# Attention turns of two rounds: the order of copies, maxima and query projections changed, and constant matmuls put into the start

## The reference, cut to what matters

```python
x = x + tanh(g_xattn[0]) * L0_xattn(layernorm(x), ctx)   # cosine similarities of two projections
x = x + tanh(g_ffn[0])   * L0_ffn(layernorm(x))          # ternary weights, rows quantised to 8 bits
x = x + tanh(g_xattn[1]) * L1_xattn(layernorm(x), ctx)   # the stage that is changed
x = x + tanh(g_ffn[1])   * L1_ffn(layernorm(x))          # 8 bit weights, one scale for the whole tensor
```

```python
q = layer_norm(x) @ Wq;  k, v = split(ctx @ Wkv)         # 16 heads, one null key and value in front
attn = softmax((q * s) @ (k * s).T, masked)              # 128 x 129 per head and batch
out  = layer_norm((attn @ v).reshape(b, 128, 1024) @ Wout)
```

## Time and profile before

| | us |
|---|---|
| three runs | 321.82, 320.54, 321.28 (median 321.28) |
| the profiled execution, its own time | 321.2 |
| its span | 319.4 |
| PE busy | 288.1 (90%) |
| DVE busy | 256.3 (80%) |
| ACT busy | 237.7 (74%) |
| POOL busy | 157.8 (49%) |
| chain that ended last, by engine | PE 37%, DVE 26%, ACT 18%, issue 7%, POOL 6% |

### The profile page before, as it was taken

One profiled execution on the slowest core, in us unless ns is written; L12 is line 12 of the kernel. 1 busy time (PEld: TensorE's weight loads), 2 busy tenths in 40 slices (PEclk: granted clock), 3 DMA queues, 4 the chain that ended last, 5 costly groups with the idle time before them and its releaser, 6 DMA issues.

```text
span 319.4 us, 7701 instructions
## 1 busy us (share of the span) xinstructions
PE 288.1 (90%) x2594; PEld 238.7 (75%) x2594; DVE 256.3 (80%) x730; ACT 237.7 (74%) x811; POOL 157.8 (49%) x225
## 2 busy tenths in 40 slices
PE   7988999999999848999998998989999998977765
PEld 6767768686767637889998998989889887842455
DVE  3798999999886446667887888988889889858875
ACT  2777696869899665898888897888978886419290
POOL 2124617342442114645578797867857586443200
PEclk9999999999999995999999999999999999999999
DMA  5741000002020000000000000000000000000004
GB/s 156 180 127 27 1 25 3 3 0 66 3 66 3 0 0 0 2 3 3 0 3 2 2 1 3 2 0 3 3 3 2 1 2 2 1 2 0 1 2 131
DMA packets 11479, 6.67 MB, mean 21 GB/s; under 512 B 3825, under 2 KB 10993, under 8 KB 11441
## 3 DMA queue, kind: packets, MB, share of 16 engines
q1 hardware_dynamic: 10560, 5.99, 6.9%
q10 hardware_dynamic: 880, 0.20, 0.3%
HBM read 5.14 MB, written 1.05 MB: 19 GB/s over the span
## 4 chain that ended last, share of the span: by engine, by line
PE 37%; DVE 26%; ACT 18%; issue 7%; POOL 6%; DMA 3%; SPq 2%; ACTq 0%; DVEq 0%; POOLq 0%
PE psum L1074 10%; DVE rmx L2023 9%; ACT work L1005 8%; PE psum L1078 6%; PE psum L1080 5%; PE psum L1079 5%; DVE den L2038 3%; POOL work L584 3%; DVE work L2016 2%; ACT late L1005 2%; DMA KT<-in_L_ffn_w_down 2%; DVE hgm L2221 2%; ACT work L1065 2%; PE psum L1539 2%; PE psum L1202 2%
## 5 line engine op out<-in xcount | busy, mean ns | idle before, releaser
L584 POOL TENSOR_TENSOR work<-work,rden 128x512 f32<-128x512 f32 x51 | 52.9, 1040 | 43.3 <-DVE rden L2042 43.3
L1005 ACT ACTIVATE work<-psum,nmx 128x128 f32<-128x128 f32 x208 | 73.3, 383 | 0.0
L1074 PE MATMUL psum<-ident,work 128*128 128x128 f32 (+2 forms) x328 | 49.9, 285 | 7.1 <-DVE work L2016 4.8
L1074 PEld LDWEIGHTS psum<-ident,work 128*128 128x128 f32 (+2 forms) x328 | 37.5, 145 | 16.1 <-issue 8.8
L1005 ACT ACTIVATION_READ_ACCUMULATOR work<-psum,nmx 128x1 f32 x208 | 46.7, 225 | 0.0
L2023 DVE TENSOR_REDUCE rmx<-psum 128x8 f32<-128x1024 f32 x32 | 38.6, 1208 | 5.0 <-PE psum L1202 5.0
L1202 PE MATMUL psum<-KT,work 64*128 64x128 f32 x512 | 35.5, 288 | 5.9 <-ACT work L1005 5.0
L2038 DVE SCALAR_TENSOR_TENSOR den<-null_exp,masked,key_sum 128x4 f32<-128x4 f32 x64 | 22.6, 353 | 20.6 <-ACT work L1005 15.9
L1202 PEld LDWEIGHTS psum<-KT,work 64*128 64x128 f32 x512 | 31.9, 193 | 9.1 <-issue 8.1
L1078 PE MATMUL psum<-split 128*128 128x256 f32 (+1 forms) x96 | 37.3, 389 | 1.3 <-issue 0.8
L1080 PE MATMUL psum<-split 128*128 128x256 f32 (+1 forms) x96 | 31.0, 323 | 0.0
(11 more groups left out here) (216 smaller groups left out, 757.4 us busy)
## 6 DMA issues: line engine op xcount, KB each, us to landing
KT<-in_L_xattn_Wkv SPq DMA_DIRECT2D x2, 384.0 KB, 4.7
X<-in_x SPq DMA_DIRECT2D x1, 768.0 KB, 5.8
out_x<-X SPq DMA_DIRECT2D x3, 256.0 KB, 2.6
work<-in_ctx SPq DMA_DIRECT2D x3, 192.0 KB, 2.4
work<-in_L_xattn_Wq SPq DMA_DIRECT2D x1, 512.0 KB, 3.6
work<-in_L_xattn_Wout SPq DMA_DIRECT2D x1, 512.0 KB, 3.9
X<-in_x SPq DMA_DIRECT2D x1, 256.0 KB, 3.5
KT<-in_L_ffn_w_gate SPq DMA_DIRECT2D x1, 256.0 KB, 5.7
```

Source lines behind the costliest of these rows:

```text
L584: pool.tensor_tensor(sx_, sx_, bcast(rden[n % 2][:, :], S), ALU.mult).then_inc(p_ready.sem, 1)
L1005: ins = act.activation(Sx[n % 5][:, j, :], bank[2 * (r % 2) + j % 2][:, at * S:(at + 1) * S], ACT.Exp, bias=nmx[r % 2][:, col:col + 1], ac ...
L1074: return pe.transpose(dst, src, ident[0:m, 0:m])
```

## The change

On PE, the second query projection of a turn now stands in front of the odd transposes. On DVE, the maxima of the odd round stand behind the copies of the even transposes of the next turn, and both copies of the odd transposes stand in front of the denominator of unit new + 1. In turn 0 and turn 1, PE gets 22 and 2 constant matmuls, and the transposes of round 0 move from turn 2 into turn 1. In the last turn one `pair_work` moves behind the last copies.

```diff
             for M in range(NT + 1):
-                both(round_transposes, 2 * M - 4)
+                if M > 2:
+                    both(round_transposes, 2 * M - 4)
                 queries(2 * M)
                 both(out_proj, 2 * M - 6)
+                queries(2 * M + 1)
                 both(round_transposes, 2 * M - 3)
-                queries(2 * M + 1)
                 both(out_proj, 2 * M - 5)
...
                 both(round_scores, 2 * M)
+                if M == 1:
+                    keep_clock_long(bank[5], 2)
+                    both(round_transposes, 0)
                 both(round_scores, 2 * M + 1)
+                if M == 0:
+                    keep_clock_long(bank[5], 22)
...
                     p_evac(old + 1)
                 if new >= 0:
+                    maxima(2 * M - 1)
                     denominators(new)
                 if old >= 0:
                     p_evac(old + 2)
+                    p_evac(old + 3)
                 if new >= 0:
                     denominators(new + 1)
-                if old >= 0:
-                    p_evac(old + 3)
                 if M == NT:
                     p_evac(NS - 4)
                 pair_work(2 * M)
                 if new >= 0:
                     denominators(new + 2)
-                pair_work(2 * M + 1)
+                if M < NT:
+                    pair_work(2 * M + 1)
                 if new >= 0:
                     denominators(new + 3)
                 if M < NT:
                     maxima(2 * M)
-                    maxima(2 * M + 1)
             last_normalise()
             p_evac(NS - 3)
             p_evac(NS - 2)
+            pair_work(2 * NT + 1)
```

## The result

The changed kernel takes 332.85 us in the median of four runs, against 321.55 for the kernel before beside it; the ratio is 1.0263, with a 95% interval from 1.0167 to 1.0359. Two of the four runs were disturbed ones, the profiled one (334.53 us, span 332.7) among them, and the ratio leaves them out; 321.55 times 1.0263 is 330.0 us.

A forecast was written before the change was run, and what follows sets the result against it. It took PE's 9.38 us per turn plus waits as the bound before, and two longer loops through ACT, DVE and POOL after. Start -1.8, turns 3 to 6 +1.0, turns 7 to 15 +7.9, tail 0: 321.2 + 7.1 = 328.3 us, range 325.3 to 330.5.

The forecast's parts named there:

- What bounds the kernel: Middle turns: PE's floor is 9.38 us, turns take 9.82, and the 0.44 above is waiting, nearly 4 us to win.
- The start, -1.8: Up to turn 2's maxima: earlier transposes and queries let ACT copy at 125.50, saving 1.8 us, bounds -2.2 and -0.6.
- The rival on the constants: Turn 2: the clock stays slow despite constants, the start gives 0.6 not 1.8, 329.5 us; chance inside the forecast's 0.68.
- no slow slice: Sign of being right at the start: even maxima of turn 2 at about 131.8 us and no slice at slow clock.
- Turns 3 to 6, +1.0: Early turns without the full POOL queue: 39.1 us against 38.1, so +1.0, between -0.4 and +1.5.
- Turns 7 to 15, the loops, +7.9: Late queries and denominator delay POOL's queue and the next maxima: loops of 10.69 (even) and 10.79 us (odd), +7.9.
- The rule on DVE and POOL: Odd turns: DVE and POOL exclude each other, so next_norm's stall stays; without it odd loops are about 0.8 us shorter.
- The clock, a rival at 0.06: PE gaps of 1 to 2 us drop its clock, 9.4 us becoming up to 18 in some turns: 333 us and more; 0.06.
- The tail, 0: Last turn: moved pair_work frees 0.7 us of DVE, but PE waits for POOL's normalise: 0, bounds -0.7 and +0.7.
- The meant gain, 315.5 at 0.11: Rival: the new loop doesn't reach POOL's queue and turns fall to near PE's floor: -5.7, 315.5 us; chance 0.11.

The follow-up runs named there:

- e4: The changed kernel with odd transposes back before the second queries and the denominator of unit new + 1 back between the odd copies: 316.12 us, ratio 0.9840.
- e10: The kernel before with one edit on DVE, the odd maxima moved behind the even copies: 318.09 us, ratio 0.9896.
- e12: e4 with the statistics of x half a turn later for the first five pairs: 314.55 us, ratio 0.9798 to the kernel before.
- e1: The changed kernel run once more with no edit: 330.67 us against 320.69 for the kernel before, ratio 1.0272.
- e6: The kernel before with only the new start (constant matmuls, transposes of round 0 in turn 1): 319.96 us, ratio 0.9957.
- e7: The changed kernel without its 24 constant matmuls: 329.45 us, ratio 1.0264 to the kernel before.
- e9: The changed kernel with four constant matmuls before the second queries in odd turns 7 to 15: 329.56 us, ratio 1.0254 to the kernel before.
- e11: The changed kernel with POOL's first pair_work of a turn in front of the normalise of unit new + 1: 325.47 us, ratio 1.0121 to the kernel before.
- e3: The changed kernel with the denominator of unit new + 1 back between the two odd copies: 322.82 us, ratio 1.0062 to the kernel before.
- e5: The changed kernel with eight constant matmuls before the second queries in turns 7 to 15: 332.66 us, ratio 1.0361 to the kernel before.

## Why the prediction was right, and where it was off

*What bounds the kernel.* Half right. The floor of 9.38 us was right, and so was the milestone view. But the prediction put the 0.44 us above the floor down to PE's wait for DVE's copy in all turns. That holds for the odd ones, which fell from 9.95 to 9.67 us when the wait was lifted (e4). The even turn of 9.82 us is already the loop through POOL: 5.99 + 2.56 + 1.27. All three numbers stood in the prediction, as parts of the new loop, and were not added up for the old one. In e4 and e10 even turns kept their length without that wait, and in e12 they fell to 8.87 when the statistics left the loop.

*The start, -1.8.* Right: -1.84 in e1, -1.6 alone in e6. The reason was half right: the queries come earlier, but the constants add nothing (e7). The rival on the constants priced their failure at 1.2 us; what they protect was hidden by ACT's exponents. Where the clock fell behind the next gap of 1.85 us, the start took 17.9 us and not 16.9. That was so in the first run of the change, where the sign "no slow slice" failed, and not in e1.

*Turns 3 to 6, +1.0.* +1.5 in e1, at the upper bound: turn 3 and turn 6 were set down 0.5 and 0.4 us too short.

*Turns 7 to 15, the loops, +7.9.* Right in size and in mechanism. Even turns 10.73 us against 10.69, odd ones 10.76 against 10.79, and the intermediate marks of turns 8 and 11 within 0.04. e9, where no turn is slow, has +7.6 in all. PE's wait moved to line 1078. It is 0.2 to 0.4 us long in turns 4 to 6, and 1.1 to 1.9 in turns 7 to 15, but for the two turns behind the slow ones with 0.4 and 0.2. `residual` is late, and e11 shows that the loop runs through it.

*The rule on DVE and POOL.* By the Trainium skill, SBUF — State Buffer, section Who interferes with whom, the stall of `next_norm` was to stay. The trace agrees: in turn 9 after it took 1.06 us, from just behind the start of a `normalise` (207.75) to just behind its end, and in turn 8, where it began ahead of one, 0.34; the denominator behind it took 0.95 there and ended at 194.73, with POOL's `normalise` at 194.72. The odd turns came out at 10.8 and not 0.8 shorter. No run here takes the stall away by itself, so that the port is its cause is not shown.

*The clock, a rival at 0.06.* This is the step that failed, though the forecast held. The prediction said that no row shows a clock that fell in a gap under 2 us. That was true of the rows, but the longest such gap it had was 1.16 us, and the change made gaps of 1.9. The clock fell in two turns of nine. The price was wrong the other way: not "up to 18" us for a turn but 11.5 to 11.7. In turn 9 after, PE comes to the values 3.33 us behind the start of the transposes and not 1.86, so it is 1.5 us late. But the loop takes from PE only the transposes, which make the `normalise` of unit new + 1 0.87 us later; the rest goes into the gap of turn 10, 0.35 us and not 1.11, in which PE would have waited anyway. It adds 1.65 us to the sum, and with +0.5 in turns 3 to 6 and -0.3 in the loops it makes the +8.9 of e1's stretches out of the predicted +7.1. That the last two nearly cancel is luck, and small. The Trainium skill, TensorE: Matmul & The Clock Gate, section HAM oscillation, warns of waits that throttle PE again in loops that alternate work and waiting. The trace agrees in turn 9, with 0.85 granted. But the waits in the example of the Trainium skill are longer than the 1.92 us here, and turn 11 had the same gap and a granted clock of 1.00.

*The tail, 0.* Right.

*The meant gain, 315.5 at 0.11.* It is near what a kernel without the two reorderings gives (e4, 316.12), though by another way, with turns of 9.6 us and not at PE's floor. So the idea of the change, maxima behind the copies, was sound, and worth 3.3 us alone (e10). The two other edits took 14 us from it.

## What to carry to other kernels

Add up the loop that the kernel runs in now, from one milestone of a turn to the same one a turn later, through every engine it touches, before reading an engine's idle time as what can be won: if a chain that doesn't contain that wait already has the turn's length, removing the wait brings little. Two reorderings that are cheap alone can be dear together when one's instruction waits for what the other has put late, so they are measured one at a time. Where a change lengthens a gap of PE beyond the longest one in the trace, give a fall of its clock a real chance, and price only the slow work that lies on the loop; what fills PE's own waiting costs nothing.

## What the runs showed of the hardware

A gap of 1.84 to 1.92 us on PE is sometimes followed by the slow clock and sometimes not, in the same place of the same kernel: behind 1.84 us in turn 2 of e1 it held (eight transposes 1.03 us),

```profile
125.74 0.36 PE L1078 MATMUL psum<-split 128*128 128x256 f32 x1 [1.84 <-ACT work L993]
...
126.52 1.03 PE L1074 MATMUL psum<-ident,work 128*128 128x128 f32 x8
```

and behind 1.85 us in turn 2 of the first run of the change it fell (1.91 us):

```profile
130.01 0.36 PE L1078 MATMUL psum<-split 128*128 128x256 f32 x1 [1.85 <-ACT work L993]
...
130.98 1.91 PE L1074 MATMUL psum<-ident,work 128*128 128x128 f32 x8
```

There are 18 gaps of 1.84 to 1.92 us in the profiled runs of this stage (the change, e1, e3, e5, e7, e9 and e11), and behind nine of them the clock fell. It doesn't fall with the gap: in turn 9 of the first run of the change the first four matmuls of the queries still take 0.28 to 0.36 us, and the fifth, 0.55 us behind the end of the gap, is the first that takes longer, 0.38; in turn 13 all six are at full clock and the eight transposes behind them take 1.54 us, so the fall came among these. Behind gaps up to 1.42 us (e11) and one of 1.64 (e6) the clock stayed full, where it was full before. What decides between the two at 1.9 us stays open.
